# Four buffers for the row of statistics, FFN weight in 28 pieces, and ScalarE's exponentials placed first

## The reference, cut to what matters

```python
def conv(x):                       # triangle multiplication
    xn = layer_norm(x, norm_a, norm_b)
    left  = (xn @ Wl + bl) * sigmoid(xn @ Wlg + blg)
    right = (xn @ Wr + br) * sigmoid(xn @ Wrg + brg)
    gate  = sigmoid(xn @ Wog + bog)
    out = einsum('bkjd,bkid->bijd', left, right) / n
    return (layer_norm(out, on_a, on_b) * gate) @ Wo + bo

def ffn(t):                        # 64 experts, each picks its 8 best tokens
    probs = softmax(einsum('bsd,ed->bse', t, gate_w) + gate_b, axis=tokens)
    vals, idx = top_k(probs over the tokens, 8)
    h = gelu([pooled tokens, 1] @ weight1)       # per expert, 129 x 512
    out = [h, 1] @ weight2                       # per expert, 513 x 128
    return scatter_add(out * vals at idx)

x = x + conv(ln(x));  t = tokens(x);  t = t + ffn(ln(t))
```

## Time and profile before

| what | value |
|---|---|
| median of 3 runs | 3089.35 us (3086.25 to 3095.03) |
| the profiled execution | 3078.97 us, span 3077.0 us |
| stage 1 | to about 1145 us |
| stage 2 | about 1145 to 1850 us |
| stage 3 | about 1880 to 2960 us |
| tail | about 2960 to 3077 us |
| busy in the whole span | PE 84%, DVE 79%, ACT 77%, POOL 61% |

### The profile page before, as it was taken

How to read it: one execution, slowest core, us unless ns; L and a number is a source line. 1 busy time by engine, 2 the same in 40 slices (tenths; PEclk the granted TensorE clock), 3 DMA queues, 4 the chain that set the end, 5 groups by cost and what they waited for, 6 DMA issues and landing times.

```text
span 3077.0 us, 66113 instructions
## 1 busy us (share of the span) xinstructions
PE 2588.5 (84%) x14998; PEld 2145.9 (70%) x15070; DVE 2428.7 (79%) x4824; ACT 2363.5 (77%) x4284; POOL 1889.3 (61%) x2343
## 2 busy tenths in 40 slices
PE   7999999999999989989998984777777777777735
PEld 6888888888888878888988983555555555555523
DVE  6777777777777769999999996778777787787862
ACT  6888888888888877887878872888778787787850
POOL 8888888888888860000000003888788887887842
PEclk9999999999999999999999996999999999999967
DMA  5777777777777769999999985888888888888836
GB/s 199 270 267 268 267 270 273 270 269 269 267 268 268 270 256 318 333 327 325 343 330 325 332 295 185 301 309 307 297 300 309 303 299 298 309 309 297 303 139 202
DMA packets 281154, 873.00 MB, mean 284 GB/s; under 512 B 29223, under 2 KB 81602, under 8 KB 281122
## 3 DMA queue, kind: packets, MB, share of 16 engines
q1 hardware_dynamic: 272322, 855.31, 77.2%
q10 hardware_dynamic: 8448, 16.78, 1.6%
q0 software_dynamic: 352, 0.53, 0.2%
HBM read 492.97 MB, written 379.52 MB: 284 GB/s over the span
## 4 chain that ended last, share of the span: by engine, by line
PE 43%; DMA 17%; issue 14%; POOL 12%; DVE 5%; ACT 4%; SPq 2%; POOLq 1%; ACTq 0%; another core or an unknown queue 0%; DVEq 0%
PE banks L1267 32%; DMA arena<-left_d 11%; POOL rs L693 5%; DMA statrow<-stat_d 5%; POOL arena L664 4%; PE banks L1256 4%; PE banks L1335 3%; ACT arena L809 2%; PE banks L1301 1%; ACT work L879 1%; DVE left_parts L1006 1%; PE banks L1326 1%; PE banks L1336 1%; SPq L475 1%; DVE arena L1014 1%
## 5 line engine op out<-in xcount | busy, mean ns | idle before, releaser
L1267 PE MATMUL banks<-x_parts,w_parts 128*128 128x512 f32 x4320 | 1068.3, 399 | 0.8 <-POOL x_parts L626 0.8
L1267 PEld LDWEIGHTS banks<-x_parts,w_parts 128*128 128x128 f32 x4320 | 791.9, 189 | 162.9 <-POOL x_parts L626 1.2
L1301 PE MATMUL banks<-left_parts,right_parts 128*128 128x384 f32 x3456 | 629.3, 341 | 67.2 <-ACT arena L810 56.8
L1301 PEld LDWEIGHTS banks<-left_parts,right_parts 128*128 128x128 f32 x3456 | 606.2, 191 | 90.5 <-issue 86.0
L957 DVE SCALAR_TENSOR_TENSOR arena<-banks,cols,arena 128x512 f32<-128x512 f32 x576 | 406.6, 747 | 255.7 <-ACT arena L775 252.3
L879 ACT ACTIVATE work<-arena,nmr,rs 128x128 f32<-128x128 f32 x1152 | 458.9, 482 | 151.9 <-POOL nmr L695 145.5
L659 POOL COPY rcol<-late 128x8 f32 (+1 forms) x144 | 28.4, 197 | 722.3 <-ACT late L825 722.3
L664 POOL TENSOR_TENSOR arena<-arena,work 128x512 f32<-128x512 f32 x288 | 359.7, 1270 | 163.1 <-DVE arena L1063 161.9
L1335 PE MATMUL banks<-wo_sb,arena 128*128 128x128 f32 x2304 | 413.3, 309 | 0.1
L1335 PEld LDWEIGHTS banks<-wo_sb,arena 128*128 128x128 f32 x2304 | 373.6, 200 | 29.4 <-issue 1.8
L626 POOL TENSOR_TENSOR x_parts<-xn,x_parts 128x512 fp32r<-128x512 f32 x288 | 372.2, 1292 | 6.6 <-ACT x_parts L763 6.6
(11 more groups left out here) (177 smaller groups left out, 4459.5 us busy)
## 6 DMA issues: line engine op xcount, KB each, us to landing
arena<-in_x_dram SPq DMA_DIRECT2D x144, 512.0 KB, 3.4
left_d<-arena SPq DMA_DIRECT2D x144, 512.0 KB, 2.6
right_d<-arena SPq DMA_DIRECT2D x144, 512.0 KB, 3.4
gate_d<-arena SPq DMA_DIRECT2D x144, 512.0 KB, 4.2
arena<-right_d SPq DMA_DIRECT2D x128, 576.0 KB, 5.8
arena<-left_d SPq DMA_DIRECT2D x128, 576.0 KB, 6.8
mixed_d<-arena SPq DMA_DIRECT2D x128, 576.0 KB, 4.2
work<-mixed_d SPq DMA_DIRECT2D x144, 512.0 KB, 4.2
```

Of the source, the lines that this page charges most:

```text
L1267: last = nc.tensor.matmul(ps[2 + k][:, :], w_parts[:, wq, k], x_parts[:, xq, b, c], start=((wq, xq) == TERMS[0]), stop=((wq, xq) == TERMS[ ...
L1301: last = nc.tensor.matmul(ps[NT * b + t][:, 0:GRID], lr_parts[RIGHT][:, rq, b, k, t * P:(t + 1) * P], lr_parts[LEFT][:, lq, b, k], start=( ...
```

## The change

Five edits go together.

1. `statrow` has four buffers `r` where it had two, with a semaphore each. `load_parts(s)` now waits for `project(s-4)` and is issued for `s+3` where it was `s+2`. TensorE's and SyncE's bodies hold four steps (`quads`), since the buffer's number must be known in the code; the other engines keep their bodies of two.
2. The tile is cleared once at the start by GpSimd, all four buffers.
3. Three small tiles of the set-up (`exact`, `exact_lo`, `exact_p`) lie in `yt`, which nothing else uses before stage 3.
4. `weight1` is loaded in 28 pieces of 512 KB, one at each of 28 cuts, and in four such pieces at the end. ScalarE's loop so falls into 29 loops of two or three bodies.
5. ScalarE does `exponentials(s-4)` after `scale_rest(s)` and before `normalise(s-1)`.

```diff
+def quads(engine, steps, body, drain=0):
+    last = steps // 4 - 1
+    body(0)
+    with engine.Fori(1, last) as j:
+        body(j)
+    for j in range(last, steps // 4 + drain):
+        body(j)
...
-        statrow = sb("statrow", [P, 2, 2, CHUNK], BF16)
+        statrow = sb("statrow", [P, 4, 2, CHUNK], BF16)
...
-            def load_parts(i, b):
-                s = 2 * i + b
-                sp.wait_ge(s_z3, mark(2, s - 2, 2))
+            def load_parts(j, r):
+                s = 4 * j + r
+                if not isinstance(j, int) or j > 0:
+                    sp.wait_ge(s_z3, mark(2, s - 4, 2))
                 settle(sp, s_tick_sp)
-                sp.dma_start(statrow[0:KR, b], stat_r[s].broadcast_to([PARTS, 2 * PARTS, 2 * CHUNK])).then_inc(s_sin[b], 16)
+                sp.dma_start(statrow[0:KR, r], stat_r[s].broadcast_to([PARTS, 2 * PARTS, 2 * CHUNK])).then_inc(s_sin[r], 16)
...
-            def stage3(i):
-                for b in range(2):
-                    if in_range(i, b, 2, STEPS):
-                        load_mixed(*shifted(i, b, 2))
-                    if in_range(i, b, -1, STEPS):
-                        store_result(*shifted(i, b, -1))
-                    if in_range(i, b, 1, STEPS):
-                        load_x3(*shifted(i, b, 1))
-                    if in_range(i, b, 2, STEPS):
-                        load_parts(*shifted(i, b, 2))
+            def stage3(j):
+                for r in range(4):
+                    if in_range4(j, r, 3, STEPS):
+                        load_parts(*shifted4(j, r, 3))
+                    if in_range4(j, r, 2, STEPS):
+                        load_mixed(*halves_of(*shifted4(j, r, 2)))
+                    if in_range4(j, r, -1, STEPS):
+                        store_result(*halves_of(*shifted4(j, r, -1)))
+                    if in_range4(j, r, 1, STEPS):
+                        load_x3(*halves_of(*shifted4(j, r, 1)))
...
             def load_w1(n):
-                for j in range(2 * n, 2 * n + 2):
-                    act.dma_start(w1_sb[:, j], w1_view[j]).then_inc(s_w1, 16)
+                j, first = n // 2, BANDS // 2 * (n % 2)
+                some = slice(first, first + BANDS // 2)
+                act.dma_start(w1_sb[:, j, some], w1_view[j, :, some]).then_inc(s_w1, 16)
...
                         scale_rest(i, b)
+                    if in_range(i, b, -4, STEPS):
+                        exponentials(*shifted(i, b, -4))
                     if in_range(i, b, -1, STEPS):
                         normalise(*shifted(i, b, -1))
                     if in_range(i, b, -2, STEPS):
                         copy_transposed(*shifted(i, b, -2))
-                    if in_range(i, b, -4, STEPS):
-                        exponentials(*shifted(i, b, -4))
-
-            cuts = [lambda n=n: load_w1(n) for n in range(WLOADS - 1)]
+
+            cuts = [lambda n=n: load_w1(n) for n in range(4 * (WLOADS - 1))]
             pairs(act, STEPS, stage3, drain=2, cuts=cuts)
...
-            load_w1(WLOADS - 1)
+            for n in range(4 * (WLOADS - 1), 4 * WLOADS):
+                load_w1(n)
...
-            def outer(i, b):
-
-                s = 2 * i + b
-                pe.wait_ge(s_sin[b], 16 * (i + 1))
+            def outer(j, r):
+                s = 4 * j + r
+                pe.wait_ge(s_sin[r], 16 * (j + 1))
...
-            pe.wait_ge(s_w1, 16 * SIDE)
+            pe.wait_ge(s_w1, 16 * 2 * SIDE)
```

More of the change, by code:

```diff
@@ L86, in pairs, with shifted4, in_range4, halves_of @@
         body(i)
+def quads(engine, steps, body, drain=0):
[5 more added lines that the diff above has]
+        body(j)
+def shifted4(j, r, k):
+    return j + (r + k) // 4, (r + k) % 4
+def in_range4(j, r, k, steps):
+    return not isinstance(j, int) or 0 <= 4 * j + r + k < steps
+def halves_of(j, r):
+    return 2 * j + r // 2, r % 2
 def build(nc, x, norm_a, norm_b, Wl, bl, Wr, br, Wlg, blg, Wrg, brg, Wog, bog, on_a, on_b, Wo, bo,
@@ L212, in build @@
         gate_t = sb("gate_t", [P, EXPERTS])
-        exact = sb("exact", [2 * PARTS, 2, DIM])
-        exact_lo = sb("exact_lo", [2 * PARTS, 2, DIM])
-        exact_p = sb("exact_p", [2 * PARTS, PARTS, 2, DIM], BF16)
+        early_rows = yt[0:2 * PARTS, 1].rearrange("p h n -> p (h n)")
+        exact = early_rows[:, 0:2 * DIM].rearrange("p (q d) -> p q d", q=2)
+        exact_lo = early_rows[:, 2 * DIM:4 * DIM].rearrange("p (q d) -> p q d", q=2)
+        exact_p = early_rows[:, 4 * DIM:(4 + PARTS) * DIM].bitcast(BF16).rearrange("p (a q d) -> p a q d", a=PARTS, q=2)
         coef = sb("coef", [P, 2, DIM], BF16)
@@ L351, in build @@
         s_x3 = [sem(f"s_x3{b}") for b in range(2)]
-        s_sin = [sem(f"s_sin{b}") for b in range(2)]
+        s_sin = [sem(f"s_sin{r}") for r in range(4)]
         s_rc = sem("s_rc")
@@ L537, in _ @@
             sp.wait_ge(s_stst, 16 * 2 * PARTS)
-            load_parts(0, 0)
-            load_parts(0, 1)
-            pairs(sp, STEPS, stage3, drain=1)
+            for r in range(3):
+                load_parts(0, r)
+            quads(sp, STEPS, stage3, drain=1)
             w2_view = weight2[:, 0:HIDDEN, :].rearrange("(g j) (p c) n -> j p g (c n)", g=BANDS, c=HC)
@@ L1317, in _, with project @@
                     nc.tensor.transpose(ps[n % 2][:, 0:P], rstd_map[:, t, c * P:(c + 1) * P], ident[:, :]).then_inc(s_rtp, 1)
-            def outer(i, b):
-                s = 2 * i + b
-                pe.wait_ge(s_sin[b], 16 * (i + 1))
+            def outer(j, r):
+                s = 4 * j + r
+                pe.wait_ge(s_sin[r], 16 * (j + 1))
                 for h in range(2):
                     pe.wait_ge(s_w3, mark(2, s - 1, h + 1))
-                    nc.tensor.matmul(ps[h][:, :], coef[:, 0, :], statrow[:, b, h, :], start=True, stop=True).then_inc(s_c3, 1)
-            def project(i, b):
-                s = 2 * i + b
+                    nc.tensor.matmul(ps[h][:, :], coef[:, 0, :], statrow[:, r, h, :], start=True, stop=True).then_inc(s_c3, 1)
+            def project(j, r):
+                s, b = 4 * j + r, r % 2
                 for h in range(2):
@@ L1335, in project @@
                         nc.tensor.matmul(ps[2 + h][:, tok], gated[:, b, h, tok], wo_sb[:, :], start=True, stop=False)
-                        last = nc.tensor.matmul(ps[2 + h][:, tok], statrow[:, b, h, tok], coef[:, 1, :], start=False, stop=True)
+                        last = nc.tensor.matmul(ps[2 + h][:, tok], statrow[:, r, h, tok], coef[:, 1, :], start=False, stop=True)
                     last.then_inc(s_z3, 1)
@@ L1354, in logits, with stage3 @@
                                      start=True, stop=True).then_inc(s_l3, 1)
[L1356 to L1365, removed]
+            def stage3(j):
+                for r in range(4):
+                    if in_range4(j, r, 1, STEPS):
+                        outer(*shifted4(j, r, 1))
+                    if in_range4(j, r, 0, STEPS):
+                        project(j, r)
+                    if in_range4(j, r, -3, STEPS):
+                        logits(*halves_of(*shifted4(j, r, -3)))
+                    if in_range4(j, r, -2, STEPS):
+                        transposes3(*halves_of(*shifted4(j, r, -2)))
             pe.wait_ge(s_rtc, NT * NT)
@@ L1370, in _ @@
             outer(0, 0)
-            pairs(pe, STEPS, stage3, drain=2)
+            quads(pe, STEPS, stage3, drain=1)
             pe.wait_ge(s_r3, mark(1, STEPS - 1, 1))
```

## The result

The changed kernel takes 2934.25 us (2932.48 to 2935.5, 4 runs) against 3092.19 us (3086.25 to 3099.24, 4 runs) before: a ratio of 0.9488, 95% interval 0.9465 to 0.9511. It is 158 us faster.

What follows compares the result with a forecast made beforehand. It took a two-step ring of waits plus holes behind `weight1` loads to bound stage 3. A pace of 6.61 us gains 111 us, less 2 of costs: 109 off the 3089.35 median, 2980 us, range 2938 to 3040.

Steps and rivals of the forecast that it cites:

- GpSimd's starts as a clock: Stage 3: GpSimd's 144 power starts give 7.385 us a step, a quiet 7.05 plus seven holes of 6.8.
- the ring: Stage 3: waits linking GpSimd, ScalarE, TensorE and VectorE over two steps, 13.97 us before, 12.9 after the change.
- three floors: Stage 3 after the change: ring 6.44 us a step, GpSimd 6.28, DMAs 6.40 to 6.83; pace taken as 6.61.
- the DMA floor: Stage 3 loads: 2.253 MB a step take 6.40 us at 352 GB/s, 6.61 at 341, 6.83 at 330.
- The rival of GpSimd: Stage 3: GpSimd is the bound at 6.28 us a step, 2933 us; chance 0.10.
- The exponential: ScalarE, stage 3: placed first, it lets logits start 0.7 us earlier and costs nothing where ScalarE waited for `nmr`.
- The buffers: `statrow` load, stage 3: some 13 us more to land, whole wait gone, `weighted` 1.1 us earlier with the earlier logits.
- The pieces: `weight1` loads, stage 3: quarter-size loads, with `statrow` given slack, remove the seven holes, 47 us.
- The sign named for them: Stage 3 profile after: no step takes 11 us or more; pieces of `weight1` make steps of under 8.
- The costs: Doubled clearing of `statrow` in set-up 1.80 us more; ScalarE's 21 further loops, longer bodies and last pieces 0.
- The DMA rival: Stage 3: the DMAs are the bound at 330 GB/s, 6.83 us a step, 3012 us; chance 0.22.
- the substitute wait: Stage 3: another wait replaces those removed, the exponential delaying `normalise`; only the holes go, 3043 us; chance 0.11.

Runs made afterwards that it cites:

- bufs_pieces: The changed kernel with the exponential last, as before: 2999.03 us, ratio 0.9713 to the kernel before.
- half_x: The changed kernel with only the first half of `x` loaded in stage 3, added to the result's second half by GpSimd: ratio 0.9489 to the kernel before.
- half_residual: The changed kernel with GpSimd adding the residual to only 256 of its 512 columns: ratio 0.9496 to the kernel before.
- half_logits_residual: The changed kernel with half the tokens left out of copy, logits, exponential and search, and GpSimd's residual on 256 of 512 columns: 2886.88 us.
- half_logits: The changed kernel with copy, logits, exponential and search on only 256 of 512 columns of each half: 2903.86 us, ratio 0.9407 to the kernel before.
- copy_first: The changed kernel with ScalarE's copy_transposed(s-2) moved before normalise(s-1): 2911.15 us, ratio 0.9421 to the kernel before.
- exp_only: The kernel before with only ScalarE's exponential moved first: 3099.64 us, ratio 1.0039.
- bufs_exp: The changed kernel with `weight1` in seven loads of 2 MB, as before: 2953.08 us, ratio 0.9561 to the kernel before.
- bufs_only: The kernel before with only the four `statrow` buffers: 3014.69 us, ratio 0.9776.
- loops_only: The kernel before with ScalarE's loop cut at 28 places, but `weight1` still in seven loads of 2 MB: ratio 0.999.
- keep_later: The changed kernel with GpSimd's keep(s-4), two copies, moved behind scales(s-1): ratio 0.9518 to the kernel before.
- pieces_only: The kernel before with only `weight1` cut into 28 pieces of 512 KB: 3143.85 us, ratio 1.0177.

## Why the prediction was wrong

**GpSimd's starts as a clock, and the ring: right.** The pace of before, the ring over two steps and its members hold. Taken by itself the ring gave 13.97 - 1.12 = 12.85 us for two steps, which the prediction rounded to 12.9 and 6.44 a step; measured are 12.84. bufs_pieces with 13.60 us for two steps and the changed kernel with 12.84 are the ring with and without the exponential.

**The step that failed: "With three floors within 0.2 us of each other the pace lies above the highest of them, and 6.61, the best rate that a row shows, is my value."** The term was mis-sized: 6.61 where 6.41 was measured, 0.20 us in each of 143 steps, 29 us. Nothing in the trace said that floors add to each other. half_x relieved the DMA engines by a ninth and half_residual relieved GpSimd, and neither moved the pace: the changed kernel runs at the length of its ring. Two things were wrong in the step. The 341 GB/s were the rate of a stage whose VectorE was busy 98.73 of 100 us, so that row more likely showed what VectorE asked for than what the DMA engines can give; the changed kernel moves 351, half_logits_residual 366. And the floors of the ring and of GpSimd, 6.44 and 6.28, were right within 0.03 us (6.41 and 6.25 were measured), while the DMA floor that I put above them was not one. With 6.44 the sum would have been (7.385 - 6.44) x 143 = 135 us, less 2: 2956 us. What was then still missing, 22.0 us, is 4.7 us of pace (6.44 against 6.407), the 6.7 us at the start and end of the stage and in stages 1 and 2, the 2 us of costs, which do not show there as a loss, and 8.6 us by which the median of before lay further above its profiled execution (10.4) than that of the changed kernel does (1.8). I saw these 10 us and took the gain off the median, but counted the gain itself from the fast execution.

**The rival of GpSimd** at 2933 us hit the time by luck and not the mechanism: its 6.28 us a step is not what the kernel does, 6.41 is, and the terms missing outside the pace made up the difference. half_logits, and by its row copy_first, are the kernels in which that rival is true.

**The exponential: right, and more than that.** It lies where ScalarE waited for `nmr`, and ScalarE's wait fell from 145.5 to 85.0 us. But alone it is worth nothing (exp_only, 0.4% slower), with the buffers 62 to 65 us by the medians (3014.69 to 2953.08, 2999.03 to 2934.25).

**The buffers: right.** They are the edit without which the others lose; alone they gave 74 us.

**The pieces: the size was wrong.** Of the 47 us forecast, 19 (bufs_exp against changed) belong to them; bufs_only against bufs_pieces gives 16, but there the intervals of the two ratios overlap. The buffers had taken the rest, since a hole was mostly the wait for `statrow`. With the old buffers the pieces cost 56 us. The sign named for them came true: no step of the changed kernel takes over 6.94 us.

**The costs.** The doubled clearing took 3.51 us where 3.6 was assumed, and ScalarE's loops cost nothing (loops_only).

**The DMA rival and the substitute wait: not seen.** VectorE waits 5.6 us in all for a load, and `normalise` still waits for `nmr` (85.0 us). GpSimd's share and that of the DMA engines came out at 0.97 and 0.97 where 0.94 and 0.96 were named.

## What to carry to other kernels

Where no engine is full, look for the ring of waits, count it over as many steps as its offsets span, and take its length as the pace: a beat over two steps in one engine's starts points to such a ring, and an engine that is relieved without changing the sum of the beat is not the bound. A floor may be taken from a row only if the resource was the limit in that row. Edits that remove waits in one ring don't add up: each alone can be worth nothing or less, so try them together before one is thrown away, and try each without the others before one is credited. Work that is moved out of a ring must go where its engine has time: keep_later moved 0.28 us of copies out of a spot where GpSimd waited anyway, and lost.

## What the runs showed of the hardware

Cutting transfers finer can cost more than it saves. With two buffers, 28 pieces of 512 KB made the kernel 1.8% slower than seven loads of 2 MB did, and the long steps stand behind the pieces (9.57 us on average) as they stood behind the loads (11.81). With four buffers the same pieces made it 19 us faster.

The DMA engines, which I took to be full at 352 GB/s, moved 359 in half_logits and copy_first, reads and writes of HBM mixed, with at most 0.4 us of waits for them in 700, and 366 in half_logits_residual, with 28.0.

TensorE's granted clock was lower in the kernels in which TensorE waits more: from 2000 to 2700 us it was 0.91 in pieces_only, 0.92 in exp_only, 0.96 before, and 1.00, the upper level of 2.4 GHz, in the changed kernel and in copy_first. The same products of `project` took 336, 324, 309 and 300 ns on average in pieces_only, exp_only, before and the changed kernel. In the kernel that waits most, the work between the waits is slower too; I had not counted that, and how much of the differences it makes was not tried.

VectorE's `minus` ended with GpSimd's gate in the steps of these timelines, however long it had run. In keep_later it took 0.79 us and ended at 2407.89, the gate at 2407.86; in the changed kernel it took 0.35 and ended at 2411.94, the gate at 2411.91. No semaphore ties the two together; why they end together was not tried.

The time of the kernel before is the less even one: 3064 to 3093 us in 10 runs beside copy_first, against 2929 to 2935 in 6 of the changed kernel. That the waits make it so is not shown.
